# A two-layer edge network: fewer, larger transfers on the SyncE queue, with three blocks of the message table in one

## The chip, the cores and the metric

One core of one Trainium2 chip runs the kernel. The metric is device time in microseconds (us), smaller is better. The kernel before took 12610.75 us as the median of three runs (12586.5 to 12617.3).

## The reference

A graph has 12500 nodes with 128 features and 412500 directed edges, sorted by their target. Layer 0 weights and sums the source rows of every node's edges and passes the sum through a small network. Layer 1 computes a filter for every edge from its 50 attributes (two linear layers with softplus), multiplies it into a row of its *target* end and sums the products by its *source* end. Both layers end in a residual and a layer norm.

```python
# layer 0, on x, src, dst, w
agg = segment_sum(w[:, None] * x[src], dst)
x = layernorm(x + relu((x + agg) @ W1 + b1) @ W2 + b2)
# layer 1
h1 = x @ lin1_w.T
c = 0.5 * (cos(w * pi / 10) + 1)
f = softplus(attr @ nn_w1.T + nn_b1) - log(2)
F = (softplus(f @ nn_w2.T + nn_b2) - log(2)) * c[:, None]
agg = segment_sum(F * h1[dst], src)
x = layernorm(x + (h1 + agg) @ lin2_w.T + lin2_b)
```

## The kernel before

Edges are cut into 403 tiles (T) of 1024 edges (TE), each of 8 groups (SUB) of 128, in two halves of 512 (HE). As the edges are sorted by target, a tile's targets lie in a window of 42 nodes (WIN), rarely in more than one.

The kernel runs in stages, each a block in which every engine has a program of its own, in order, and engines meet by semaphores. `wait_apart` is a semaphore wait followed by an increment of a counter of its own; `prime` is a tiny DMA that starts a semaphore off.

**First layer's edges** (lines 357 to 605). For each tile GpSimd gathers source rows with 8 indirect DMAs (line 433) into `xg`. TensorE sums them with a weighted one-hot (L473) into a window of `aggT`, which VectorE adds up (L498). The same loop prepares layer 1: TensorE multiplies the tile's attributes, `attr` (51 rows with a row of ones, two buffers of 512 edges), with the first filter matrix (L479), ScalarE makes the softplus (L396 to L400), VectorE puts it into `hid` (two buffers, L505), and SyncE stores it to `hidden` in HBM (L365). VectorE and TensorE also compute every edge's place in a table sorted by source bucket (buckets of 128 nodes). The edges form 4 parts; in each part a bucket has a run of whole blocks of 512 rows. The last block of a run is only partly filled, so SyncE clears a block for it ahead of time (L381). SyncE's program for one tile is: two loads of `attr`, two stores of `hid`, one clear. `PT` is 101 tiles, a part.

**First layer's nodes** (`layer0_nodes`) writes, among others, `h1_parts`: the rows of h1 as three bfloat16 parts (128 columns each) that add up to float32.

**Second layer's edges** (`layer1_edges`, from L944). For each tile, SyncE loads `e_hid` (two halves, L1009), the targets `dstb` (L1017, the same row for all partitions) and the window's h1 rows `h1w` (L1020): 3 x 42 rows, one DMA for each of the three parts, one part below the other. TensorE computes the second filter layer (L1077, L1080), ScalarE the softplus (L1135 to L1139), VectorE the one-hot `ohT` (L1223), TensorE picks and adds the three parts of h1 (`take_h1`, L1091), VectorE finishes the messages (L1238, L1245) and GpSimd scatters the message rows with 8 indirect DMAs into the sorted table (L1199). A table row has 132 numbers: the message, its place in the bucket, and its factor c.

105 tiles (`alone`) run like this. From then on, in the third loop (298 tiles, two to an iteration), a *turn* of three blocks (`TURN`) is summed beside each tile: SyncE reads their row numbers from `slot_row` (`find_blocks`, L1026), loads the three blocks (`load_blocks`, L1038, 264 KB each, into one of two sets of three buffers), VectorE and ScalarE build one-hots from the rows' places (L1273, L1167 and L1169), TensorE sums (`sum_turn`, L1111) and VectorE adds the sum into `aggT` (`add_turn`, L1285). The blocks of a turn always are neighbours in the table, and a turn never crosses a part. After the last tile some 90 turns follow, without tiles (the last loop).

SyncE's order for one tile of the third loop is: `load_hidden` (two waits on `z2_set`, two DMAs), `find_blocks` for the next turn (three register loads), `written` (two waits until scattered rows have landed), `load_blocks` (three times: a wait on `summed1`, so that the block's buffer is free, and a DMA), `load_windows` (a wait and the DMA of `dstb`, a wait and three DMAs of `h1w`). TensorE's order is: second filter layer, `take_h1`, `sum_turn`. VectorE's is: `ohT`, messages, then for each of the three blocks `add_turn`'s add and the next turn's one-hot. ScalarE's is: softplus, then the next turn's one-hots.

**Second layer's nodes** writes the output.

Of the kernel before, what the change touches and what calls it, by code (L numbers as in the profile page):

```python
# [51 lines left out]
def edge_network_kernel(nc, x_rows, x_cols, src_cols, dst_cols, w_cols, dst_rows,  # L52
# [8 lines left out]
    with ctx:  # L61
# [3 lines left out]
        def sem(name):  # L65
            return ctx.enter_context(nc.semaphore(name))
# [240 lines left out]
        with ExitStack() as c1:  # L307
# [3 lines left out]
            with ExitStack() as c2:  # L311
# [13 lines left out]
                attr = [sb2(f"attr{h}", [P, HE], f32) for h in range(2)]  # L325
                soft1 = [sb2(f"soft1_{h}", [P, HE], f32) for h in range(2)]
                hid = [sb2(f"hid{h}", [P, HE], f32) for h in range(2)]
# [12 lines left out]
                attr_padded, attr_in = sem("attr_padded"), [sem(f"attr_in{h}") for h in range(2)]  # L340
                z1_set, abs1, exp1, ln1, hid_set = (sem(n) for n in ("z1_set", "abs1", "exp1", "ln1", "hid_set"))
                hid_st = [sem(f"hid_stored{h}") for h in range(2)]
# [11 lines left out]
                with nc.Block() as block:  # L354
                    @block.sync
                    def _(sp):
# [5 lines left out]
                        def store_hidden(t, h):  # L362

                            wait_apart(sp, hid_set, taken_up(t, h), passed_sp)
                            sp.dma_start(hid_d[ds(t, 1), h, :, :].rearrange("o p e -> (o p) e"), hid[h][:, :]).then_inc(hid_st[h], 16)  # L365

                        for h in range(2):
                            prime(sp, spare[16 + h:17 + h, :], hid_st[h], zero)
                        sp.wait_ge(attr_padded, 2)
# [12 lines left out]
                        for h in range(2):  # L382
                            store_hidden(T, h)
                        for h in range(2):
                            sp.wait_ge(hid_st[h], 16 * (T + 2))
                        sp.wait_ge(blocks_cleared, 16 * T)
# [53 lines left out]
                    def _(pe):  # L440
# [16 lines left out]
                        for q, first, past_last in parts:  # L457
                            plan_part(q)
                            with pe.Fori(first, past_last) as t:
# [16 lines left out]
                                for h in range(2):  # L476
                                    pe.wait_ge(attr_in[h], 16 * (t + 1))
                                    pe.wait_ge(hid_set, taken_up(t, h))
                                    nc.tensor.matmul(bank[2 + h][:, :], nn1[:, :], attr[h][:, :], start=True, stop=True).then_inc(z1_set, 1)  # L479
# [966 lines left out]
```

## Time and profile before

| | us |
|---|---|
| median of three runs | 12610.75 |
| the profiled execution | 12679.28 |
| its span, first to last instruction | 12677.7 |
| PE busy | 6363.2 (50%) |
| DVE busy | 6551.5 (52%) |
| ACT busy | 4527.6 (36%) |
| POOL busy | 6390.3 (50%) |

PE is TensorE's matmuls, PEld its weight loads, DVE VectorE, ACT ScalarE, POOL GpSimd and SP SyncE. `SPq` is SyncE's sequencer, which issues DMAs. A span covers one core. The granted TensorE clock had a mean of 0.64 of full speed, and the DMA engines moved 121 GB/s over the span. A wait is put down to what released it; "remote" stands where an update came late that the profile can't put down to an instruction just before it.

### The profile page before, as it was taken

The numbers are of one execution on the slowest core, as the hardware profiler recorded it, in microseconds if no ns is written. First come the engines' busy times: TensorE is split into PE (matmuls) and PEld (weight loads), VectorE is DVE, ScalarE is ACT, GpSimd is POOL, SyncE is SP. The second block draws the span as 40 slices with busy tenths as digits, with TensorE's granted clock in tenths as the row PEclk, the third lists the DMA queues.
The fourth block names the chain that finished last, engine by engine and source line by source line (L and its number), as shares of the span: only waits on it lengthen the run. The fifth ranks groups of instructions, "written<-read, shape, count | busy, mean of one in ns | idle before, by whom it ended". The sixth has DMA issues, their size and how long they took to land. (4 is left out here: it accounts for less than half of the span.)

```text
span 12677.7 us, 208085 instructions
## 1 busy us (share of the span) xinstructions
PE 6363.2 (50%) x29276; PEld 4956.9 (39%) x29548; DVE 6551.5 (52%) x18326; ACT 4527.6 (36%) x9921; POOL 6390.3 (50%) x6542
## 2 busy tenths in 40 slices
PE   2555566655665555553333444444444444444457
PEld 1333333333333333343333344444444444444457
DVE  7666666666666555543333344444444444444457
ACT  2333333333333333343333333333333333333347
POOL 3666666566666666625555444444444444444430
PEclk7555555555555555575565666666666666666678
DMA  3333333333333333333333444444444444444456
GB/s 99 117 118 118 116 121 120 116 120 116 121 118 120 119 114 117 116 121 99 100 101 100 123 123 123 123 123 124 123 122 123 124 122 124 124 122 122 122 151 202
DMA packets 864996, 1531.32 MB, mean 121 GB/s; under 512 B 235294, under 2 KB 249044, under 8 KB 864460
## 3 DMA queue, kind: packets, MB, share of 16 engines
q1 hardware_dynamic: 655168, 1091.59, 28.2%
q0 software_dynamic: 209456, 436.16, 11.6%
q10 hardware_dynamic: 348, 3.33, 0.1%
q14 instruction: 18, 0.15, 0.0%
q8 instruction: 6, 0.10, 0.0%
HBM read 967.92 MB, written 562.42 MB: 121 GB/s over the span
## 5 line engine op out<-in xcount | busy, mean ns | idle before, releaser
L1199 POOL DMA_INDIRECT sorted_messages<-rows,sidx x3224 | 3101.1, 962 | 3756.4 <-DVE sidx L1241 1776.6
L433 POOL DMA_INDIRECT xg<-x_rows,gidx x3224 | 3247.3, 1007 | 2118.2 <-issue 1040.1
L473 PE MATMUL bank<-onehot,xg 128*128 128x42 f32 x6448 | 1564.2, 396 | 1546.0 <-DMA xg<-x_rows,gidx 649.6
L473 PEld LDWEIGHTS bank<-onehot,xg 128*128 128x128 f32 x6448 | 1366.1, 298 | 1742.2 <-issue 972.4
L1091 PE MATMUL bank<-h1w,ohT 128*128 128x128 bf16 x3224 | 398.4, 301 | 3123.7 <-DMA h1w<-h_parts 1680.3
L479 PE MATMUL bank<-attr,nn 128*128 128x512 f32 x1612 | 1551.8, 1101 | 552.3 <-DMA attr<-attr_cols 402.9
L1111 PE MATMUL bank<-hot,block_rows 128*128 128x128 f32 x9312 | 1656.8, 357 | 41.3 <-DVE hot L1273 18.3
L1111 PEld LDWEIGHTS bank<-hot,block_rows 128*128 128x128 f32 x9312 | 1614.9, 270 | 56.1 <-issue 41.1
L1091 PEld LDWEIGHTS bank<-h1w,ohT 128*128 128x128 bf16 x3224 | 306.4, 137 | 3193.6 <-DMA h1w<-h_parts 3162.3
L1080 PE MATMUL bank<-w_nn2T,e_hid 128*128 128x128 f32 x6448 | 1044.0, 314 | 680.3 <-DMA e_hid<-hidden 606.7
L1080 PEld LDWEIGHTS bank<-w_nn2T,e_hid 128*128 128x128 f32 x6448 | 1004.1, 226 | 641.5 <-DMA e_hid<-hidden 547.2
L396 ACT ACTIVATE soft<-bank 128x512 f32<-128x512 f32 x808 | 477.0, 590 | 2152.1 <-remote 1254.6
L1135 ACT ACTIVATE soft<-bank 128x512 f32<-128x512 f32 x806 | 481.1, 597 | 2045.3 <-remote 1790.3
L1223 DVE TENSOR_SCALAR ohT<-dstb,rel 128x1024 bf16<-128x1024 int16 x403 | 199.6, 495 | 1935.1 <-DMA dstb<-dst 1770.3
L1167 ACT ACTIVATE hot<-cols,block_rows 128x128 f32<-128x128 f32 x1167 | 467.2, 400 | 1769.9 <-remote 875.7
L1273 DVE TENSOR_SCALAR hot<-neg_cols,block_rows 128x128 f32<-128x128 f32 x3501 | 1018.8, 359 | 4.6 <-DMA block_rows<-sorted_messages 4.6
L1285 DVE TENSOR_TENSOR aggT<-aggT,bank 128x128 f32 x1164 | 329.3, 283 | 1079.0 <-remote 715.7
L479 PEld LDWEIGHTS bank<-attr,nn 128*128 128x128 f32 x1612 | 447.4, 319 | 1068.4 <-issue 862.9
L1238 DVE SCALAR_TENSOR_TENSOR filt<-bank,soft 128x512 f32<-128x512 f32 x806 | 555.7, 689 | 550.3 <-ACT soft L1139 370.7
L1245 DVE TENSOR_TENSOR rows<-filt,bank 128x512 f32<-128x512 f32 x806 | 553.9, 687 | 401.3 <-remote 302.2
L561 DVE TENSOR_TENSOR onehot<-cols,rel 128x336 f32<-128x336 f32 x403 | 203.0, 504 | 971.6 <-remote 904.8
L412 ACT ACTIVATE gidx<-srci 128x4 int32 x806 | 165.5, 205 | 1401.5 <-DMA xg<-x_rows,gidx 820.3
(184 smaller groups left out, 8712.5 us busy)
## 6 DMA issues: line engine op xcount, KB each, us to landing
block_rows<-sorted_messages SPq DMA_DIRECT2D x1167, 264.0 KB
hidden<-hid SPq DMA_DIRECT2D x808, 256.0 KB
e_hid<-hidden SPq DMA_DIRECT2D x806, 256.0 KB
sorted_messages<-zero SPq DMA_DIRECT2D x403, 264.0 KB
dstb<-dst SPq DMA_DIRECT2D x403, 256.0 KB
attr<-attr_cols SPq DMA_DIRECT2D x806, 102.0 KB
xg<-x_rows,gidx POOLq DMA_INDIRECT x3224
sorted_messages<-rows,sidx POOLq DMA_INDIRECT x3224
```

The source lines that it names most:

```text
L396: nc.scalar.activation(soft1[h][:, :], bank[2 + h][:, :], ACT.Abs).then_inc(abs1, 1)
L433: pool.indirect_dma_start(xg[s][:, :], None, x_rows, bass.IndirectOffsetOnAxis(ap=gidx[s // HALF][:, s % HALF:s % HALF + 1], axis=0),).the ...
L473: nc.tensor.matmul(bank[0][:, 0:WIN], xg[s][:, :], onehot[:, s, :], start=(s == 0), stop=(s == SUB - 1)).then_inc(summed, 1)
L479: nc.tensor.matmul(bank[2 + h][:, :], nn1[:, :], attr[h][:, :], start=True, stop=True).then_inc(z1_set, 1)
L1080: ins = nc.tensor.matmul(bank[2 + h][:, s * P:s * P + P], hid[h][:, s * P:s * P + P], nn2T[:, :], start=False, stop=(s == HALF - 1))
L1091: ins = nc.tensor.matmul(bank[4 + h][:, s * P:s * P + P], ohT[:, at:at + P], h1w[:, :], start=True, stop=True)
L1111: ins = nc.tensor.matmul(sums[u][:, 0:P], block_rows[k][u][:, s, 0:D], hot[u][:, s, :], start=(s == 0), stop=(s == HALF - 1))
L1135: nc.scalar.activation(soft2[h][:, :], bank[2 + h][:, :], ACT.Abs).then_inc(abs2, 1)
L1199: pool.indirect_dma_start(table, bass.IndirectOffsetOnAxis(ap=sidx[h][:, s:s + 1], axis=0), rows[h][:, s, :], None).then_inc(landed[h], 16)
L1238: dve.scalar_tensor_tensor(filt[h][:, :], bank[2 + h][:, :], 0.0, soft2[h][:, :], ALU.max, ALU.add).then_inc(filt_set, 1)
L1245: dve.tensor_tensor(rows[h][:, :, 0:D], filt[h][:, :].rearrange("p (s d) -> p s d", s=HALF), bank[4 + h][:, :].rearrange("p (s d) -> p s d ...
L1273: ins = dve.tensor_scalar(hot[u][:, s, :], neg_cols[:, :], mine[:, s, D:D + 1], mine[:, s, D + 1:D + 2], ALU.is_equal, ALU.mult)
```

## The change

The pairs of buffers `attr`, `hid` and `e_hid` become one buffer each with the halves side by side, loaded or stored in one DMA; a set of three blocks becomes one buffer, loaded in one DMA from the first block's row; the three parts of the h1 rows come in one DMA with a rearranged source. Waits are on the later half, or on the third block's sum. Since a turn's three blocks are now read even where only the first is used, two more blocks behind each part's last are cleared, in four DMAs at the end of the first layer's edges. TensorE's matmuls, VectorE's and ScalarE's operations are the same apart from the waits and the buffers' names.

```diff
@@ first layer's edges, SyncE
-                        def store_hidden(t, h):
-
-                            wait_apart(sp, hid_set, taken_up(t, h), passed_sp)
-                            sp.dma_start(hid_d[ds(t, 1), h, :, :].rearrange("o p e -> (o p) e"), hid[h][:, :]).then_inc(hid_st[h], 16)
+                        def store_hidden(t):
+
+                            wait_apart(sp, hid_set, taken_up(t, 1), passed_sp)
+                            sp.dma_start(hid_d[ds(t, 1), :, :, :].rearrange("o h p e -> p (o h) e"), hid[:, :, :]).then_inc(hid_st, 16)
...
-                                for h in range(2):
-                                    wait_apart(sp, z1_set, made(t, h), passed_sp)
-                                    sp.dma_start(attr[h][0:GAUSS + 1, :], attr_cols[:, ds(t * TE + h * HE, HE)]).then_inc(attr_in[h], 16)
-                                for h in range(2):
-                                    store_hidden(t, h)
+                                wait_apart(sp, z1_set, made(t, 1), passed_sp)
+                                sp.dma_start(attr[0:GAUSS + 1, :, :].rearrange("a h e -> a (h e)"), attr_cols[:, ds(t * TE, TE)]).then_inc(attr_in, 16)
+                                store_hidden(t)
...
+                        store_hidden(T)
+                        for q in range(PARTS):
+
+                            sp.reg_load(end, ends[0:1, q * PT + NB:q * PT + NB + 1])
+                            row = sp.snap(end, min_val=0, max_val=TABROWS - BLOCK)
+                            sp.dma_start(sorted_d[q // TABLE_PARTS][ds(row, 2 * BLOCK), :].rearrange("(k p g) d -> p k (g d)", k=2, p=P),
+                                         zero[:, :].rearrange("p (o e) -> p o e", o=1).broadcast_to([P, 2, 4 * RW])).then_inc(blocks_cleared, 16)
@@ first layer's edges, TensorE and VectorE
-                                    pe.wait_ge(attr_in[h], 16 * (t + 1))
+                                    pe.wait_ge(attr_in, 16 * (t + 1))
...
-                            dve.wait_ge(hid_st[h], 16 * (t + 1))
+                            dve.wait_ge(hid_st, 16 * (t + 1))
@@ second layer's edges, SyncE
-                for h in range(2):
-                    wait_apart(sp, z2_set, freed(j, h), passed_sp)
-                    sp.dma_start(hid[h][:, :], hid_d[ds(t + 1, 1), h, :, :].rearrange("o p e -> (o p) e")).then_inc(hid_in[h], 16)
+                wait_apart(sp, z2_set, freed(j, 1), passed_sp)
+                sp.dma_start(hid[:, :, :], hid_d[ds(t + 1, 1), :, :, :].rearrange("o h p e -> p (o h) e")).then_inc(hid_in, 16)
...
-                    for k in range(3):
-                        sp.dma_start(h1w[WIN * k:WIN * (k + 1), :], h1_parts[ds(node, WIN), k * D:(k + 1) * D]).then_inc(h1w_in, 16)
+                    sp.dma_start(h1w[0:KEEP, :], h1_parts[ds(node, WIN), :].rearrange("r (k d) -> k r d", k=3)).then_inc(h1w_in, 16)
...
             def find_blocks(c, k):
-                for u in range(TURN):
-                    sp.reg_load(at[u], slot_row[0:1, ds(first_slot(c, k) + u, 1)])
+                sp.reg_load(at, slot_row[0:1, ds(first_slot(c, k), 1)])
...
-                for u in range(TURN):
-                    row = sp.snap(at[u], min_val=0, max_val=TABROWS - BLOCK)
-                    if used:
-                        wait_apart(sp, summed1, first_slot(c, k) + u + 1 - TURN, passed_sp)
-                    sp.dma_start(block_rows[k][u][:, :, :].rearrange("p g d -> p (g d)"),
-                                 table[ds(row, BLOCK), :].rearrange("(p g) d -> p (g d)", p=P)).then_inc(block_in[k][u], 16)
+                row = sp.snap(at, min_val=0, max_val=TABROWS - TURN * BLOCK)
+                if used:
+                    wait_apart(sp, summed1, first_slot(c, k), passed_sp)
+                sp.dma_start(block_rows[k][:, :, :, :].rearrange("p u g d -> p u (g d)"),
+                             table[ds(row, TURN * BLOCK), :].rearrange("(u p g) d -> p u (g d)", u=TURN, p=P)).then_inc(block_in[k], 16)
@@ second layer's edges, VectorE (ScalarE's hot_turn alike)
-                dve.wait_ge(block_in[k][u], 16 * (c + 1))
+                if u == 0:
+                    dve.wait_ge(block_in[k], 16 * (c + 1))
```

## Rows read from the trace of the kernel before

**Rows 1.** stages: us, busy PE, PEld, DVE, ACT, POOL, PEclk, DMA share, GB/s

```profile
166.00:5377.00 5211.00, 3086.12 (x8865) 1886.88 (x8865) 3373.24 (x6670) 1619.48 (x3209) 3235.53 (x3213) 0.56 0.38 118
...
5573.00:7010.00 1437.00, 519.45 (x2637) 454.60 (x2741) 455.67 (x1589) 452.31 (x1065) 807.31 (x840) 0.59 0.33 101
...
7010.00:12246.00 5236.00, 2281.28 (x14698) 2206.89 (x14845) 2131.25 (x8014) 2013.20 (x4742) 2285.61 (x2376) 0.69 0.42 123
...
12246.00:12574.00 328.00, 282.49 (x2192) 267.69 (x2192) 275.50 (x1097) 235.42 (x553) 8.15 (x9) 0.97 0.73 225
```

**Rows 2.** waits of the third loop: us in total, times, longest

```profile
DVE ohT L1223 <- DMA dstb<-dst: 1534.1, 276, 11.2
...
PE bank L1091 <- DMA h1w<-h_parts: 1476.3, 159, 10.7
...
DVE aggT L1285 <- remote: 712.8, 145, 10.6
```

**Rows 3.** timeline of one tile: start us, us, engine, line, operation, idle before

```profile
9000.29 4.64 PE L1111 MATMUL bank<-hot,block_rows 128*128 128x128 f32 x24
...
9001.75 0.96 POOL L1199 DMA_INDIRECT sorted_messages<-rows,sidx  x1 [6.22 <-ACT rows L1146]
...
9005.26 7.94 SPq L1038 DMA_DIRECT2D block_rows<-sorted_messages  x3
...
9011.92 0.29 DVE L1285 TENSOR_TENSOR aggT<-aggT,bank 128x128 f32 x1 [5.85 <-remote]
...
9013.55 0.34 SPq L1017 DMA_DIRECT2D dstb<-dst  x1
...
9016.68 0.49 DVE L1223 TENSOR_SCALAR ohT<-dstb,rel 128x1024 bf16<-128x1024 int16 x1 [3.55 <-DMA dstb<-dst]
...
9020.57 0.96 POOL L1199 DMA_INDIRECT sorted_messages<-rows,sidx  x1 [9.02 <-DVE sidx L1241]
```

**Rows 4.** timeline of the tile behind it

```profile
9018.22 4.23 PE L1111 MATMUL bank<-hot,block_rows 128*128 128x128 f32 x24
...
9029.46 0.96 POOL L1199 DMA_INDIRECT sorted_messages<-rows,sidx  x1 [0.30 <-issue]
...
9032.29 0.60 ACT L1135 ACTIVATE soft<-bank 128x512 f32<-128x512 f32 x1 [7.93 <-remote]
...
9034.33 0.69 DVE L1238 SCALAR_TENSOR_TENSOR filt<-bank,soft 128x512 f32<-128x512 f32 x1 [3.15 <-ACT soft L1139]
...
9036.72 0.96 POOL L1199 DMA_INDIRECT sorted_messages<-rows,sidx  x1 [6.30 <-ACT rows L1146]
```

**Rows 5.** one line of SyncE in the third loop: ns min/median/max

```profile
L1038 SPq MOVE block_rows<-sorted_messages x891: 3/29/1396, 7012.5 to 12239.3; - x179
```

**Rows 6.** first layer's edges: waits, then two places of SyncE's timeline

```profile
PE bank L479 <- DMA attr<-attr_cols: 402.9, 154, 5.4
...
3003.05 7.07 SPq L375 DMA_DIRECT2D attr<-attr_cols  x2
...
3015.68 0.95 SPq L375 DMA_DIRECT2D attr<-attr_cols  x2
```

**Rows 7.** waits of the second layer without sums

```profile
PE bank L1091 <- DMA h1w<-h_parts: 194.1, 31, 13.3
```

**Rows 8.** DMA queue from 12300 to 12550, and the timeline of the last loop

```profile
q1 hardware_dynamic: 31717, 59.55, 78.3%
...
12403.12 1.01 SPq L1038 DMA_DIRECT2D block_rows<-sorted_messages  x2
...
12404.20 2.98 PE L1111 MATMUL bank<-hot,block_rows 128*128 128x128 f32 x24 [0.22 <-DVE aggT L1285]
...
12407.68 4.50 PE L1111 MATMUL bank<-hot,block_rows 128*128 128x128 f32 x33 [0.50 <-DVE hot L1273]
...
12405.96 0.40 ACT L1167 ACTIVATE hot<-cols,block_rows 128x128 f32<-128x128 f32 x1 [0.26 <-DMA block_rows<-sorted_messages]
```

**Rows 9.** DMA queue in the microsecond 9033 to 9034

```profile
q1 hardware_dynamic: 112, 0.02, 10.3%
```

More of the change, by code:

```diff
@@ L324, in edge_network_kernel @@
                 hits = sb2("hits", [P, PART_COLS], bf16)
-                attr = [sb2(f"attr{h}", [P, HE], f32) for h in range(2)]
+                attr = sb2("attr", [P, 2, HE], f32)
                 soft1 = [sb2(f"soft1_{h}", [P, HE], f32) for h in range(2)]
-                hid = [sb2(f"hid{h}", [P, HE], f32) for h in range(2)]
+                hid = sb2("hid", [P, 2, HE], f32)
                 cnt_i, blocks_i = sb2("bucket_rows_i", [P, 1], i32), sb2("bucket_blocks_i", [P, 1], i32)
@@ L486, in _ @@
                         dve.sem_inc(bucket_counts, NB)
-                        for h in range(2):
-                            dve.memset(attr[h][:, :], 0.0).then_inc(attr_padded, 1)
+                        dve.memset(attr[:, :, :], 0.0).then_inc(attr_padded, 1)
                         def wide(ap, n):
@@ L952, in layer1_edges @@
     ALU, ACT, ds = mybir.AluOpType, mybir.ActivationFunctionType, bass.ds
-    hid = [sbuf(f"e_hid{h}", [P, HE], f32) for h in range(2)]
+    hid = sbuf("e_hid", [P, 2, HE], f32)
     soft2 = [sbuf(f"soft2_{h}", [P, HE], f32) for h in range(2)]
@@ L961, in layer1_edges @@
     off, away, aside = (sbuf(n, [P, SUB], f32) for n in ("off", "away", "aside"))
-    block_rows = [[sbuf(f"block_rows{k}{u}", [P, HALF, RW], f32) for u in range(TURN)] for k in range(2)]
+    block_rows = [sbuf(f"block_rows{k}", [P, TURN, HALF, RW], f32) for k in range(2)]
     hot = [sbuf(f"hot{u}", [P, HALF, P], f32) for u in range(TURN)]
     sums = [bank[0], bank[1], bank[6]]
-    hid_in = [sem(f"hid_in{h}") for h in range(2)]
+    hid_in = sem("hid_in")
     dstb_in, h1w_in = sem("dstb_in"), sem("h1w_in")
@@ L971, in layer1_edges @@
     passed, passed_sp = sem("e_passed_pool"), sem("e_passed_sp")
-    block_in = [[sem(f"block_in{k}{u}") for u in range(TURN)] for k in range(2)]
+    block_in = [sem(f"block_in{k}") for k in range(2)]
     hotD_set, hotA_set, dist_set, summed1, added = (sem(n) for n in ("hotD_set", "hotA_set", "dist_set", "summed1", "added"))
@@ L997, in _ @@
             jobs = TileTable(sp, "sp1", nwin, base)
-            at = [sp.alloc_register(f"sp1_block_row{u}") for u in range(TURN)]
+            at = sp.alloc_register("sp1_turn_row")
             begun = [sp.alloc_register(f"sp1_begun{k}") for k in range(4)]
@@ L1086, in take_h1 @@
                 pe.wait_ge(oh_set, j + 2)
[L1087 removed]
+                pe.wait_ge(h1w_in, 16 * (j + 1))
                 pe.wait_ge(msg_set, freed(j, h))
@@ L1110, in sum_turn @@
                     for s in range(HALF):
-                        ins = nc.tensor.matmul(sums[u][:, 0:P], block_rows[k][u][:, s, 0:D], hot[u][:, s, :],
+                        ins = nc.tensor.matmul(sums[u][:, 0:P], block_rows[k][:, u, s, 0:D], hot[u][:, s, :],
                                                start=(s == 0), stop=(s == HALF - 1))
```

32 lines of the change are left out of this document (14 added, 18 removed).

## The prediction

> **What bounds the kernel now.** I read the stages first [rows 1]. The profiled execution took 12679.28 us (span 12677.7), 68.5 us above the median of the three timed runs (12610.75). Four loops make up nearly all of it: the first layer's edges (403 tiles in 5211 us, 12.93 us a tile), the second layer's edges without sums (105 tiles in 1437 us, with the start of the stage), the same with sums (298 tiles in 5236 us, 17.57 us a tile) and sums alone (90 turns in 328 us). No engine is busy for more than two thirds of any of the first three, and the DMA engines for at most 0.42, so waits bound them.
>
> Next come the waits of the third loop [rows 2], then one pair of its tiles in order of time [rows 3, 4]. GpSimd scatters a tile's messages in eight indirect DMAs, 0.96 us each and 0.30 us apart, in one burst of 9.8 us (from 9001.75 to about 9011.55). What counts is the gap until the next burst. The reader is to see that the other engines stand still for the later part of a burst. TensorE's sums end at 9004.93 (9000.29 + 4.64), yet VectorE adds the last of them at 9011.92, 0.4 us after the burst, after 5.85 us of idle time put down to "remote": the update of `summed1` arrives only then. SyncE needs 7.94 us there to issue three block loads. How often: VectorE stood in this way for 712.8 us in 145 places [rows 2], so in about half of the 298 tiles. SyncE's shortest instruction shows the same: a MOVE has a median of 29 ns in this loop, but takes up to 1396 ns [rows 5]. I take from it that a SyncE instruction inside a burst costs about 0.7 us (7.94 us for some eleven of them), and that a semaphore update that isn't through some 2.5 to 3 us after the burst began is held to its end.
>
> So there are two kinds of tile. In the held kind [rows 3] the last block load waits for the held update, `dstb` is issued at 9013.55, `ohT` is built at 9016.68, and the next burst begins at 9020.57, 9.0 us after the last. In the other [rows 4] the burst ends at 9030.42, ScalarE gets its input, held as well, at 9032.29, VectorE gets the softplus at 9034.33, and the next burst starts at 9036.72: a gap of 6.3 us, ended by the softplus chain. There `h1w` arrives just in time.
>
> **The change part by part.** All sums are against the profiled time.
>
> 1. *Sums alone* (90 turns). Now a block may load as soon as its own third of the buffer is free. Afterwards 792 KB come in one DMA that waits for all three sums of the turn before. A load issued at 12403.12 releases ScalarE at 12405.96, 2.84 us later [rows 8]. Two blocks more in it cost from nothing (if its fixed part dominates) to 2 x 264 KB at 238 GB/s = 2.3 us. I take 1.6 us: 16 more packets for each of 16 engines at 99 ns (78.3% of 16 x 250 us over 31717 packets). So 0.15 us of wait and issue plus 4.4 us. After landing come VectorE's first one-hot and three blocks at the present pace (3.48 us for a turn, from 12404.20 to 12407.68, so 1.16 us each) with a fourth step to fill the chain: 4.3 us or so. The chain spans two turns, as there are two buffers: (0.15 + 4.4 + 4.3) / 2 = 4.4 us a turn, against 3.5 now. 90 x 0.9 = **+80 us** (bounds: with 2.84 us it is 3.65 a turn, +15 us; with 2.3 us more it is 4.8, +117 us).
>
> 2. *The third loop.* SyncE loses five of nine DMAs a tile (one of `e_hid`, two of the blocks, two of `h1w`), with their moves and waits, and two of three register loads. In a tile that isn't held the two spared `h1w` issues are worth 1.15 us. Of these about 0.5 us is lost to the larger `h1w` DMA, and the softplus chain lets only 0.25 us of the rest through: 153 x -0.25 = -38 us. The second block's instructions are hidden, since the wait for the third sum comes after them. In a held tile the one block DMA leaves after the burst, directly ahead of `dstb`, for which everything waits there. Now one block is ahead of it. Two more cost 1.3 us (bounds: 0, if they don't delay `dstb`; 2.3 us at 238 GB/s). The held share may change too: with `h1w` earlier, the sums start up to 0.4 us earlier against the burst, and their ends are spread around the limit (3.2 us after the start of a burst, held [rows 3]; 9018.22 + 4.23 against 9020.57, 1.9 us, not held [rows 3, 4]). I let a quarter of the 145 turn: 109 x 1.3 = +142, 36 x (6.3 - 9.0) = -97, 189 x -0.25 = -47. Together **0 us**; with no tile turned it is +150 us, with all turned -392 - 75 = -467 us.
>
> 3. *First layer's edges.* SyncE issues three DMAs a tile instead of five. TensorE waited for `attr` 402.9 us in 154 places. While gathers run, the two `attr` DMAs take 7.07 us to issue, otherwise 0.95 us [rows 6]; the second is what is late. One DMA leaves at the time of the first, with twice the rows' bytes. Most of those waits lie inside bursts, where TensorE's update would be held anyway. Outside them the spared issue of the `hid` store brings `attr` up to 0.7 us forward on TensorE's chain. I count a quarter of the 402.9 us: **-100 us** (bounds: all of it, -403 us; and +160 us, if the first half, no longer a DMA of its own, is 0.4 us late in all 403 tiles). The store of `hid` waits for both halves; VectorE needs the buffer again some 8 us later, so nothing waits for that.
>
> 4. *Second layer without sums.* TensorE waits for `h1w` 194.1 us in 31 places [rows 7], mostly on issues drawn out inside bursts; two of three go. Softplus inputs are held there as well. **-40 us** (bounds -194 us, and +74 us if the joined `e_hid` lands 0.7 us later for the first half in all 105 tiles).
>
> 5. *Four clears of two blocks* at the end of the first layer's edges: four issues and 4 x 528 KB behind the last store, 9.1 us at 238 GB/s, partly beside the other engines' last tile. **+5 us** (bounds 0 and +9). The single `memset` of `attr` runs once; the merged waits of ScalarE and VectorE stand beside their idle time.
>
> Sum: 80 + 0 - 100 - 40 + 5 = **-55 us**, 12624 profiled and 12555 in the timed runs.
>
> In the microsecond 9033 to 9034 only `h1w` is moved: 112 packets take 10.3% of 16 engines, so 15 ns each [rows 9]. The Trainium skill (DMA: Bandwidth & Descriptors, "Why a DMA increments its semaphore by 16 and not by 1") says that a DMA is split over the largest number of engines, up to 16, that divides the slowest dimension of both sides. By that rule 42 rows used 14 engines, and the new shape, 126 rows against 3 parts, uses 3: 42 rows on an engine instead of 9 in all. At 15 ns that is 0.5 us, as taken above. No view here shows the split itself.
>
> **The rivals.**
> - *Held tiles vanish.* If SyncE's lighter queue lets the sums get ahead of the limit, half to all of the 145 go to the 6.3 us gap. Half: 72 x -2.7 + 73 x 1.3 + 225 x -0.25 = -156 us, with the other parts -211, **12400**; all: -522, 12089. For it: less than 1 us decides in a tile. Against it: ScalarE's input stays held in both kinds.
> - *The big transfer stands in the way (slower).* Place: the SyncE queue just after a burst, in held tiles. Price: at 1.3 us and half of the gains of parts 3 and 4, 188 + 85 - 38 - 70 = +165, **12776**; at 2.3 us and no such gains, 333 + 85 - 38 = +380, 12991. It decides where the third sum's update comes after the burst and VectorE's wait for `dstb` (1534.1 us in 276 places [rows 2]) is the last one.
> - *All is hidden but the last loop.* SyncE's spared instructions lay beside held updates in every loop: 80 + 5, **12696**. For it: ScalarE's held input [rows 4].
> - *Few engines for `h1w`.* If a small row costs what a packet of a block costs (99 ns), 33 more on an engine are 3.3 us, less 1.15 us, in the 190 tiles where TensorE waited for `h1w` (159 and 31 [rows 2, 7]): +409 - 55, **12965**. The page's rule at its worst price; the 15 ns speak against it.
>
> **How the numbers follow.** The forecast has 0.45 (its own range 12450 to 12680), the vanished tiles 0.20, all hidden 0.15, the big transfer 0.14, few engines 0.06. A measurement of this kernel tells 0.3% (38 us) from no change. Of the forecast's 0.45, 0.27 is faster, 0.11 within, 0.07 slower; the vanished tiles are faster; of all hidden 0.03 is within and 0.12 slower; the other two are slower. That makes 0.47, 0.14 and 0.39. The range leaves a tenth on each side: 12330 to 12810.
>
> **What would show it.** Right: four SyncE DMAs a tile in the third loop; fewer than 145 "remote" waits of the add; a turn near 4.4 us in the last loop, with waits of VectorE or ScalarE for `block_rows`; `attr` waits well under 403 us. Wrong: a last loop that stays at 3.5 us a turn; a first loop that keeps its 12.9 us a tile; a third loop far from 17.6 us a tile either way; `h1w` waits that grow.

## The result and the profile after

The changed kernel took 11919.75 us (median of 4 runs, 11847.79 to 11946.0) beside 12598.62 us of the kernel before on the same chip: a ratio of 0.9453, interval 0.9407 to 0.9498. That is 679 us less; the forecast was 55 us less, and the range did not reach it. The profiled execution took 11847.79 us, 831.5 us less than the profiled one before.

The stages of the kernel after (columns as in [rows 1]; first layer, second layer without sums, third loop, sums alone):

```profile
163.00:5233.00 5070.00, 2908.76 (x8868) 1850.32 (x8869) 3380.04 (x6671) 1614.86 (x3210) 3257.62 (x3213) 0.59 0.39 122
5434.00:6821.00 1387.00, 550.32 (x2745) 466.13 (x2744) 454.89 (x1586) 442.87 (x1060) 809.81 (x839) 0.62 0.32 104
6821.00:11257.00 4436.00, 2377.81 (x14850) 2224.11 (x14850) 2158.87 (x8019) 1983.42 (x4752) 2298.88 (x2375) 0.74 0.46 145
11257.00:11743.00 486.00, 327.71 (x2192) 319.39 (x2192) 285.38 (x1101) 233.58 (x551) 11.49 (x12) 0.82 0.48 152
```

Against [rows 1] the first layer gained 141 us, the second layer without sums 50 us, the third loop 800 us (17.57 to 14.89 us a tile), and the last loop lost 158 us (3.6 to 5.4 us a turn, start and end included). So one term was wrong by 800 us. The waits of the third loop (us, times, longest) answer to [rows 2]:

```profile
ACT soft L1131 <- remote: 1138.3, 238, 9.0
...
PE bank L1087 <- DMA h1w<-h_parts: 770.5, 112, 9.9
...
DVE ohT L1220 <- DMA dstb<-dst: 506.6, 141, 7.2
...
DVE aggT L1283 <- remote: 175.4, 40, 10.6
```

ScalarE's line in the kernel before was

```profile
ACT soft L1135 <- remote: 1347.8, 268, 9.2
```

The held adds fell from 145 to 40, the wait for `dstb` to a third, that for `h1w` to half; ScalarE's held input fell by a sixth only. The timeline of one tile (start us, us, engine, line, operation, idle before) shows why, beside [rows 3, 4]:

```profile
9697.05 0.96 POOL L1196 DMA_INDIRECT sorted_messages<-rows,sidx  x1 [3.94 <-ACT rows L1142]
...
9697.37 0.38 SPq L1034 DMA_DIRECT2D block_rows<-sorted_messages  x1
...
9699.77 0.02 SPq L1016 DMA_DIRECT2D dstb<-dst  x1
...
9700.35 0.60 ACT L1131 ACTIVATE soft<-bank 128x512 f32<-128x512 f32 x1 [0.93 <-PE bank L1076]
...
9702.68 0.02 SPq L1018 DMA_DIRECT2D h1w<-h_parts  x1
...
9705.62 0.49 DVE L1220 TENSOR_SCALAR ohT<-dstb,rel 128x1024 bf16<-128x1024 int16 x1 [3.11 <-issue]
...
9707.16 4.08 PE L1107 MATMUL bank<-hot,block_rows 128*128 128x128 f32 x24
...
9708.59 0.60 ACT L1131 ACTIVATE soft<-bank 128x512 f32<-128x512 f32 x1 [3.25 <-remote]
...
9711.48 0.38 SPq L1034 DMA_DIRECT2D block_rows<-sorted_messages  x1
...
9711.69 0.96 POOL L1196 DMA_INDIRECT sorted_messages<-rows,sidx  x1 [4.75 <-DVE sidx L1238]
```

`dstb` leaves 2.7 us after the burst's start, `h1w` inside the burst, `ohT` is built before the burst's last DMA has ended, and TensorE is through with its sums at 9711.24, before the next burst begins. In [rows 3] `ohT` came 5.1 us after the burst. So the next block load and the next `dstb` leave in the first microseconds of the next burst too (9711.48 and 9712.40): being early hands itself on. ScalarE takes the first half of its input inside the burst, at 9700.35, and only the second half is held, to 9708.59; in [rows 4] both halves waited for the end of the burst.

I counted this for tiles 107 to 401 from the starts of `dstb` and the ends of the bursts: a tile is *late* when `dstb` is issued after the burst has ended. The kernel before has 196 late tiles of 295, the one after 41. A late tile's gap between bursts is 8.7 us on average before and 9.5 us after, any other's 5.7 and 4.2 us.

### The profile page after: what moved, and what is told of

Read it like the earlier page. It is cut to its first block and busy times, and to the rows that moved or that the text cites. A ratio compares the mean times of both kernels' runs of the same rounds, so it can differ in the third digit from the quotient of the medians.

```text
span 11846.2 us, 194081 instructions
## 1 busy us (share of the span) xinstructions
PE 6357.2 (54%) x29547; PEld 4997.1 (42%) x29548; DVE 6592.8 (56%) x18325; ACT 4480.2 (38%) x9921; POOL 6431.2 (54%) x6542
## 5 line engine op out<-in xcount | busy, mean ns | idle before, releaser
L474 PE MATMUL bank<-onehot,xg 128*128 128x42 f32 x6448 | 1480.5, 384 | 1775.0 <-DMA xg<-x_rows,gidx 881.2
L474 PEld LDWEIGHTS bank<-onehot,xg 128*128 128x128 f32 x6448 | 1303.3, 287 | 1940.3 <-DMA xg<-x_rows,gidx 979.3
L1107 PE MATMUL bank<-hot,block_rows 128*128 128x128 f32 x9312 | 1682.0, 362 | 174.2 <-DVE aggT L1283 156.5
L1107 PEld LDWEIGHTS bank<-hot,block_rows 128*128 128x128 f32 x9312 | 1640.9, 276 | 189.4 <-DVE aggT L1283 163.1
L480 PE MATMUL bank<-attr,nn 128*128 128x512 f32 x1612 | 1481.8, 1074 | 360.8 <-DMA attr<-attr_cols 335.4
L1076 PE MATMUL bank<-w_nn2T,e_hid 128*128 128x128 f32 x6448 | 1127.2, 329 | 994.8 <-DMA e_hid<-hidden 879.2
L1076 PEld LDWEIGHTS bank<-w_nn2T,e_hid 128*128 128x128 f32 x6448 | 1065.8, 239 | 1131.5 <-DMA e_hid<-hidden 967.9
L480 PEld LDWEIGHTS bank<-attr,nn 128*128 128x128 f32 x1612 | 484.3, 330 | 790.6 <-issue 607.6
```

The costliest lines, as they stand in the source:

```text
L474: nc.tensor.matmul(bank[0][:, 0:WIN], xg[s][:, :], onehot[:, s, :], start=(s == 0), stop=(s == SUB - 1)).then_inc(summed, 1)
L480: nc.tensor.matmul(bank[2 + h][:, :], nn1[:, :], attr[:, h, :], start=True, stop=True).then_inc(z1_set, 1)
L1076: ins = nc.tensor.matmul(bank[2 + h][:, s * P:s * P + P], hid[:, h, s * P:s * P + P], nn2T[:, :], start=False, stop=(s == HALF - 1))
L1107: ins = nc.tensor.matmul(sums[u][:, 0:P], block_rows[k][:, u, s, 0:D], hot[u][:, s, :], start=(s == 0), stop=(s == HALF - 1))
```

## The experiments

Eighteen runs were made, in five groups, each group on another chip; chip A is the one of the result. No chip was used for two groups. Every ratio is to the kernel before on the same chip. The chips turned out to be of two kinds, so the table comes first (third loop, last loop and late tiles of 295 from each run's trace, which is one execution):

| kernel | chip | ratio | third loop, us a tile | last loop, us | late tiles |
|---|---|---|---|---|---|
| before | A | 1 (12598.62 us) | 17.57 | 328 | 196 |
| changed | A | 0.9453 | 14.89 | 486 | 41 |
| three block DMAs | B | 0.9857 (0.9818-0.9895) | 17.30 | 325 | 190 |
| three h1w DMAs | B | 0.9889 (0.9852-0.9926) | 16.90 | 480 | 142 |
| two e_hid DMAs | B | 0.9694 (0.9644-0.9743) | 16.16 | 482 | 81 |
| first layer as before | B | 0.9666 (0.9632-0.9701) | 15.78 | 479 | 55 |
| changed, again | C | 0.9708 (0.9691-0.9726) | 16.26 | 484 | 86 |
| last loop in three | C | 0.9627 (0.9608-0.9647) | 16.38 | 324 | 88 |
| three DMAs, one wait | C | 1.0065 (1.0044-1.0085) | 18.05 | 349 | 266 |
| h1w rows interleaved | C | 0.9535 (0.9484-0.9586) | 15.25 | 480 | 26 |
| changed, third time | D | 1.0492 (1.0471-1.0513) | 12.13 | 483 | 0 |
| only the blocks | D | 1.0505 (1.0487-1.0522) | 12.26 | 482 | 0 |
| only h1w | D | 0.9996 (0.9987-1.0006) | 11.29 | 323 | 0 |
| 16 SyncE instructions | D | 1.0556 (1.0539-1.0574) | 12.29 | 479 | 0 |
| changed, fourth time | E | 0.9478 (0.9439-0.9517) | 15.02 | 481 | 32 |
| both edits | E | 0.9193 (0.9146-0.9241) | 14.65 | 324 | 21 |
| only the blocks | E | 0.9975 (0.9951-1.0000) | 16.71 | 483 | 130 |
| 16 SyncE instructions | E | 1.0117 (1.0089-1.0145) | 17.91 | 477 | 275 |
| only h1w | F | 1.0002 (0.9991-1.0013) | 11.17 | 322 | 0 |
| both edits | F | 1.0368 (1.0350-1.0386) | 12.05 | 322 | 0 |

The kernel before took 12696.21, 12743.45 and 12586.10 us on B, C and E, but 9559.26 and 9533.30 us on D and F. Its trace is there for A alone. On the four chips of the first kind the third loop's time goes with the late tiles, from 14.65 us with 21 to about 18 us with 266 and 275.

**Undoing one part (chip B).** The blocks first (this edit and those below are shortened; `row[u]` stands for the row that `at[u]` holds):

```
-                sp.reg_load(at, slot_row[.. first_slot(c, k) ..])
+                for u in range(TURN): sp.reg_load(at[u], slot_row[.. first_slot(c, k) + u ..])
-                if used: wait_apart(sp, summed1, first_slot(c, k), passed_sp)
-                sp.dma_start(block_rows[k][:, :, :, :] .., table[ds(row, TURN * BLOCK), :] ..).then_inc(block_in[k], 16)
+                for u in range(TURN):
+                    if used: wait_apart(sp, summed1, first_slot(c, k) + u + 1 - TURN, passed_sp)
+                    sp.dma_start(block_rows[k][:, u, :, :] .., table[ds(row[u], BLOCK), :] ..).then_inc(block_in[k][u], 16)
```

> The changed kernel with its three blocks loaded by three DMAs again, each with a wait and a register load of its own (the blocks' buffer and everything else as in the changed kernel). Theory (SyncE's queue): what SyncE issues in a tile of the third loop decides whether dstb and h1w leave before the GpSimd burst has slowed its instructions down; two DMAs, two loads and two waits more push dstb behind the burst again in many tiles. Then the third loop goes from 14.95 us a tile up to about 16.5 (+450 us), the last loop back from 5.15 to 3.4 us a turn (-158 us): together about +300 us against the changed kernel. Rival A (the joined h1w load alone made the gain): third loop stays near 15 us a tile, so -150 us. Rival B (the blocks alone made it): third loop back at 17.6 us a tile, +800 - 158 = +640 us.

The three `h1w` loads:

```
-  sp.dma_start(h1w[0:KEEP, :], h1_parts[ds(node, WIN), :].rearrange("r (k d) -> k r d", k=3)).then_inc(h1w_in, 16)
+  for k in range(3): sp.dma_start(h1w[WIN * k:WIN * (k + 1), :], h1_parts[ds(node, WIN), k * D:(k + 1) * D]).then_inc(h1w_in, 16)
```

> The changed kernel with the three parts of the h1 rows loaded by three DMAs again. Theory (SyncE's queue): two DMAs more a tile, issued last of a tile's loads; +1.4 us where they fall in a burst. Third loop +0.5 to +1 us a tile, +150 to +300 us, and the second layer without sums +20 to +50 us: +170 to +350 us together. Rival A (the joined h1w load made the gain): +700 us or more. Rival B (the blocks alone made it): within 50 us of the changed kernel, or faster by some tens of us, since the three DMAs spread over more engines.

The `e_hid` loads of the second layer:

```
-  wait_apart(sp, z2_set, freed(j, 1), passed_sp); sp.dma_start(hid[:, :, :], ..).then_inc(hid_in, 16)
+  for h in range(2): wait_apart(sp, z2_set, freed(j, h), passed_sp); sp.dma_start(hid[:, h, :], ..).then_inc(hid_in[h], 16)
```

> The changed kernel with the two halves of the first layer's rows (e_hid) loaded by two DMAs again in the second layer. Theory (SyncE's queue): one DMA and one wait more, ahead of all other loads of a tile, about half the price of two: +80 to +200 us over the two loops of the second layer. Rival (what counts is only what comes between the third sum and dstb): the e_hid load is issued beside waits, so nothing, within 40 us; and faster by up to 100 us if the joined transfer, for which both halves wait, is what now ends TensorE's wait for e_hid (606.7 us before, 879.2 us after).

The first layer's `attr` loads and `hid` stores, in the same way:

```
-  wait_apart(sp, z1_set, made(t, 1), passed_sp); sp.dma_start(attr[0:GAUSS + 1, :, :] ..).then_inc(attr_in, 16)
+  for h in range(2): wait_apart(sp, z1_set, made(t, h), passed_sp); sp.dma_start(attr[0:GAUSS + 1, h, :] ..).then_inc(attr_in[h], 16)
```

> The changed kernel with the first layer's attr and hid transfers in two DMAs each again. Theory: the first layer's loop goes back from 12.61 to 12.96 us a tile, +141 us, and nothing else moves. Rival (the first layer's gain came from the run, or from elsewhere, as the code's new place): within 40 us. It is worth more than the loop's own difference only if the first layer's stage also moves the second's, for which no row speaks.

The changed kernel didn't run on B, so only the order is firm. Without the joined blocks or the joined `h1w` most of the gain is gone, with 190 and 142 late tiles; the last loop goes back to 325 us with the blocks. That joined blocks or joined `h1w` alone made the gain (rivals A and B) falls: undoing either leaves about the same, 0.986 and 0.989. `e_hid` undone left 0.969, 52 us more than the first layer undone, but with no measure of the changed kernel on B its price can't be told. For the first layer alone nothing is settled here: its loop took 12.89 us a tile undone, 12.74 to 12.88 in the other three.

**One chip is not another (chip C).**

> The changed kernel once more, unaltered, so that the other kernels of this group can be set beside it on one chip. In the first group of experiments all four kernels, also the one that differs from the changed kernel in the first layer only, ran the third loop at 15.8 us a tile or more, against 14.95 us in the changed kernel's own profile. If that came of the chip, this run has a ratio near 0.965 and a third loop of 15.5 us a tile or more; if it came of the kernels, 0.945 and 15.0 us again.

It came of the chip, or of the hour on it: 0.9708, and 16.3 us a tile.

```
+   in the last loop only: three reg_loads; for u in range(TURN): wait_apart(sp, summed1, .. + u + 1 - TURN, ..)
+       sp.dma_start(block_rows[kk][:, u, :, :] .., sorted_d[TABLES - 1][ds(row[u], BLOCK), :] ..).then_inc(tail_in[kk][u], 16)
```

> The changed kernel, but in the last loop (sums alone) the three blocks are loaded by three DMAs with waits of their own, as before; the third loop keeps its one load. Theory: the loops don't touch one another, the last loop goes from 5.15 back to 3.4 us a turn, -158 us, and all else stays: 1.2 to 1.3% faster than the changed kernel. Rival: the last loop's code and its added waits also take time elsewhere, or the last loop was slow for another reason (the held clock, contention with the last scatters): then less than 80 us.

119.84 us less than the changed kernel by the medians of C, 160 us in the last loop's own time; the third loop was 36 us longer. The theory holds for the loop.

```
    for u in range(TURN):
-       if used: wait_apart(sp, summed1, first_slot(c, k) + u + 1 - TURN, passed_sp)
+       if used and u == 0: wait_apart(sp, summed1, first_slot(c, k), passed_sp)
```

> The changed kernel with three block DMAs and three register loads again, but with the changed kernel's single wait for all three sums ahead of them. Against the kernel with three DMAs and three waits (12504.68 us, ratio 0.986) it tells whether the number of SyncE's DMAs or the number and place of its waits counts. Theory (number of SyncE's instructions issued while a burst runs): near the three-wait kernel in the third loop, 17 us a tile or more (+600 us against the changed kernel), the last loop about 4.8 us a turn. Rival (the waits: three waits on summed1 that SyncE takes up one after the other, each seen late): near the changed kernel, within 100 us.

1.0065, 266 late tiles: the DMAs count, and where they stand. With three waits two of the three loads can leave before the third sum; with one wait all three stand between that sum and `dstb`, and it is 0.65% slower than the kernel before. Its last loop was expected at 4.8 us a turn and took 3.9:

```profile
12347.00:12696.00 349.00, 277.40 (x2179) 261.44 (x2180) 277.08 (x1097) 231.58 (x546) 7.68 (x8) 0.98 0.68 211
```

On this chip the last loop takes 324 us with three loads and three waits, 349 us with three loads behind one wait and 484 us with one load. So the joined wait costs 25 us, and 135 us come from joining the transfers: no block can be used before all three have landed.

```
-  sp.dma_start(h1w[0:KEEP, :], h1_parts[ds(node, WIN), :].rearrange("r (k d) -> k r d", k=3))
+  sp.dma_start(h1w[0:KEEP, :], h1_parts[ds(node, WIN), :].rearrange("r (k d) -> r k d", k=3))
   (and pidx, the row that a partition stands for, is p // 3 in place of p - 42k)
```

> The changed kernel with the rows of h1w laid out interleaved (row 3r+k in place of 42k+r; the one-hot's partition index is changed to match, at no cost in the loops), so that the one h1w DMA has 42 outer rows on both sides in place of 3 against 126. Theory (the joined h1w load is moved by few DMA engines and lands some 0.5 us later than it could): TensorE's wait for h1w (801.3 us in the profile after) shrinks, third loop -0.1 to -0.5 us a tile, -30 to -150 us. Rival (h1w is late by its issue, not by its transfer): within 30 us. Other rival (small descriptors are the same price however spread): the same.

245.8 us less than the changed kernel on C by the medians (1.8% by the ratios). TensorE's wait for `h1w` in the third loop, the changed kernel first:

```profile
PE bank L1087 <- DMA h1w<-h_parts: 1361.3, 163, 10.6
```

```profile
PE bank L1090 <- DMA h1w<-h_parts: 817.0, 136, 9.3
```

The gain is larger than the 30 to 150 us that I allowed, and not for the reason I gave. The issue on SyncE is shorter (ns min/median/max; changed kernel on D, then both edits on F):

```profile
L1018 SPq DMA_DIRECT2D h1w<-h_parts x288: 850/866/880, 5906.8 to 9399.6; - x144
```

```profile
L1023 SPq DMA_DIRECT2D h1w<-h_parts x289: 382/388/391, 5908.6 to 9392.5; - x145
```

and on D and F, where no burst is slow, TensorE's weight loads wait as long for `h1w` (1344.4 and 1374.9 us in all) and start 4.78 and 4.75 us after the issue on average, so it lands no earlier to speak of. On C the issue's median in the third loop fell from 722 to 388 ns, and 60 tiles moved from late to not late (86 to 26). That the shorter issue did this is a reading; no run there tells it from an earlier landing inside bursts.

**Where no burst is slow (chip D).**

> The changed kernel once more, as the measure for the other three of this group on their chip. Its ratio to the kernel before was 0.945 on one chip and 0.971 on another; if it lies with the chip and not with single executions, the four runs here agree within 1% and the ratio falls between 0.94 and 0.975.

> Of the change only the blocks' part (three blocks in one transfer, and the four clears of two blocks); h1w in three DMAs, e_hid, attr and hid in two, as in the kernel before. Theory (threshold: each step that SyncE spares before dstb and h1w moves tiles from 'dstb issued after the burst' to 'inside it', and the parts help each other): alone it brings the third loop from 17.6 to about 17.2 us a tile (-120 us) and costs 158 us in the last loop: ratio 0.99 to 1.005. Rival (the parts are independent, the blocks carry most): -400 us, ratio 0.965 to 0.975.

> Of the change only the h1w part (and the four clears). Theory (parts help each other): third loop from 17.6 to about 17.3 us a tile, -90 us, second layer without sums -20 us: ratio 0.985 to 0.995, and the gains of the parts alone add up to less than half of the whole change's. Rival (independent, h1w carries most): ratio 0.965 to 0.975. With few DMA engines as the mechanism (h1w lands later) it would be slower than before, above 1.00.

```
+                    for _ in range(8): sp.sem_inc(passed_sp, 1); sp.reg_mov(idle, 0)
                     wait_apart(sp, oh_set, j + 1, passed_sp)
                     sp.dma_start(dstb[:, :], dst16[ds(t, 1), :] ..
```

> The changed kernel with 16 instructions more on SyncE in each tile of the second layer, right before the wait for the one-hot that precedes dstb: 8 semaphore increments and 8 register moves, no DMA and no transfer. It tells whether it is SyncE's instructions or its DMAs that set dstb late. Theory (each SyncE instruction issued while GpSimd's burst runs takes about 0.7 us, and 0.03 us outside): 16 of them are up to 11 us inside a burst, so dstb falls behind the burst in most tiles and the third loop goes to 17.5 us a tile or more (+500 us or more over the changed kernel on this chip), dstb issued after the burst in over half of the tiles. Rival (only DMA issues or their transfers count): 16 instructions at 0.03 us, 0.5 us a tile at most, within 60 us.

Of the four only the rival of the last came true (57.4 us, "within 60"), and I did not expect such a chip: the kernel before took 9559.26 us, and the changed kernel was 4.9% slower. One line of SyncE in the third loop tells the kinds of chip apart (ns min/median/max): the changed kernel on A, then on D.

```profile
L1008 SPq MOVE e_hid<-hidden x295: 5/39/1393, 6824.5 to 11249.1; - x148
```

```profile
L1008 SPq MOVE e_hid<-hidden x294: 29/39/39, 5848.7 to 9438.8; - x147
```

On D no instruction of SyncE is drawn out, no wait of the third loop is "remote", and no tile is late. There the change has nothing to mend and its price shows. Beside the kernel with only `h1w` joined, which takes as long as the kernel before, it is 160 us in the last loop and 252 us in the third (12.13 against 11.29 us). The blocks' part alone brings it all (1.0505). In the third loop that price is, by the waits, `dstb` behind the big block load. The kernel with only `h1w` joined, then the changed one, both on D:

```profile
8003.83 2.28 SPq L1041 DMA_DIRECT2D block_rows<-sorted_messages  x3
8006.66 0.34 SPq L1021 DMA_DIRECT2D dstb<-dst  x1
...
8011.16 0.49 DVE L1226 TENSOR_SCALAR ohT<-dstb,rel 128x1024 bf16<-128x1024 int16 x1 [1.90 <-DMA dstb<-dst]
```

```profile
8007.40 0.38 SPq L1034 DMA_DIRECT2D block_rows<-sorted_messages  x1
...
8008.32 0.35 SPq L1016 DMA_DIRECT2D dstb<-dst  x1
...
8013.05 0.49 DVE L1220 TENSOR_SCALAR ohT<-dstb,rel 128x1024 bf16<-128x1024 int16 x1 [3.61 <-DMA dstb<-dst]
```

From the issue of `dstb` to `ohT` it is 4.50 us and 4.73 us in these tiles, and over the loop the waits are

```profile
DVE ohT L1226 <- DMA dstb<-dst: 501.4, 267, 3.7
```

```profile
DVE ohT L1220 <- DMA dstb<-dst: 812.2, 295, 4.8
```

311 us more. The mean delay from the issue of `dstb` to `ohT` is 4.15 and 4.73 us, so 0.6 us a tile is put down to the transfer ahead; `dstb` also leaves 0.4 us later after the start of the burst. The kernel with 16 instructions more bears this out: its `dstb` leaves 0.57 us later behind the block load, but `ohT` comes only 0.17 us later behind it. No run had `dstb` ahead of the blocks.

**The same on a chip with slow bursts (chip E).**

> The changed kernel as the measure for the other three of this group. If the chip is one with slow bursts (the kernel before near 12600 to 12750 us): ratio 0.945 to 0.971. If it is one without (before near 9560 us): 1.049 again, since then it is the chip and not the hour that decides.

> The changed kernel with two edits tried singly before: the last loop's three blocks in three DMAs (0.8% there over the changed kernel), and h1w's rows interleaved so that its one DMA has 42 outer rows on both sides (1.8%). Theory (the two touch different loops, so they add): 2.5% faster than the changed kernel where bursts are slow, 0.92 to 0.95 of before. Where they are not: -158 us for the last loop and nothing for h1w, 1.6% faster than the changed kernel, so still 1.03 of before. Rival (they don't add, h1w_spread's gain was one chip's scatter): 0.8% only.

> Of the change the blocks' part alone (and the four clears). Where bursts are slow: theory (parts help each other past a threshold): third loop between the kernel before and the changed kernel, nearer to before: 0.98 to 1.005. Rival (independent parts, blocks carry most): 0.955 to 0.975. Where they are not: 1.05 again.

> The changed kernel with 16 register and semaphore instructions more on SyncE ahead of the wait for dstb. Where bursts are slow: theory (each SyncE instruction in a burst costs about 0.7 us): dstb behind the burst in over half of the tiles, third loop 17.5 us a tile or more, +400 us or more over the changed kernel. Rival (only DMAs count): within 100 us. Where bursts are not slow: +57 us over the changed kernel again, since 16 instructions take 0.5 us.

Here are the two clearest results. The blocks alone gain nothing in all that can be told from zero (0.9975, interval to 1.0000). That is the net of two loops: against the kernel before on A the third loop is 0.86 us a tile shorter, 258 us, which is between the 120 us of the theory and the 400 us of the rival, and the last loop takes 155 us back. On B the joined blocks were worth 1.52 us a tile beside the other parts (17.30 against 15.78 us), so the parts help each other, as far as two chips can be compared. And the 16 instructions, 57 us on D, cost 827.7 us on E: SyncE's instructions set `dstb` late without any DMA. The rival (only DMAs count) falls. In one tile of that kernel:

```profile
9001.46 0.95 POOL L1200 DMA_INDIRECT sorted_messages<-rows,sidx  x1 [6.80 <-DVE sidx L1242]
...
9005.59 0.40 SPq L1038 DMA_DIRECT2D block_rows<-sorted_messages  x1
...
9013.93 0.01 SPq L1020 DMA_DIRECT2D dstb<-dst  x1
...
9015.95 0.49 DVE L1224 TENSOR_SCALAR ohT<-dstb,rel 128x1024 bf16<-128x1024 int16 x1 [9.23 <-DMA dstb<-dst]
...
9019.88 0.96 POOL L1200 DMA_INDIRECT sorted_messages<-rows,sidx  x1 [6.62 <-DVE sidx L1242]
```

8.3 us from the block load to `dstb`, where the changed kernel needs 0.92 us on D and 2.4 us in the tile of A above. Both edits together give 314.7 us over the changed kernel (2.6%; 2.5% expected): the fastest kernel of the study there.

**Two more (chip F).**

> Of the change the h1w part alone (and the four clears). Where bursts are slow (the kernel before near 12600 to 12750 us): theory (parts help each other past a threshold): 0.98 to 0.998, so that blocks and h1w alone together give less than half of the whole change's 0.948 to 0.971. Rival (independent parts; what the blocks don't give, h1w does): 0.955 to 0.975. Where they are not (near 9560 us): 1.000 again.

> The fastest version so far (last loop's blocks in three DMAs, h1w's rows interleaved) on one more chip. Where bursts are slow: 0.92 to 0.945 of the kernel before. Where they are not: the last loop gives back 158 us of the changed kernel's 472 us of loss, h1w's layout nothing, so 1.033.

F is like D. `h1w` joined alone is again no change, and both edits leave 1.0368 (1.033 expected). On such chips the kernel before stays the faster one. `h1w` alone was never run on a chip with slow bursts.

## Why the prediction was wrong

*What bounds it* held: slow SyncE instructions and held updates inside bursts, on this kind of chip. That the trace of before came from one of two kinds could not be seen in it.

*Step 2, third loop* (0 us forecast, -800 us measured) is the step that failed, in three places. First the share: "I let a quarter of the 145 turn". 105 of 145 held adds went. And held adds were the wrong thing to count: the kernel with three loads behind one wait has 68 of them and that with 16 instructions more, on E, has 33, yet both run at about 18 us a tile, with 266 and 275 late tiles. What decides is whether `dstb` leaves before the burst's end. I took the sums' end against the burst's start as fixed but for 0.4 us; but it is fed back, since an early `dstb` makes an early `ohT`, early sums and an early next `dstb`. On average the third sum ended 2.7 us after the next burst's start before and 0.7 us after it now; with the 16 added instructions it was back at 2.4 us.

Second the floor: the 6.3 us gap of [rows 4], from which I also had that a tile that isn't held gains only 0.25 us, was no floor. It is the gap of a tile whose ScalarE takes neither half of its input inside the burst. Before, 78 of the 99 tiles that are not late were so, at 6.4 us on average; 10 with one half taken had 4.3 us and 11 with both had 1.3 us. After, there are 64 of the first, 133 of the second and 57 of the third, at 5.9, 4.0 and 2.7 us. So the input that I took as held in both kinds of tile came free in most. The mean gap of tiles that are not late went from 5.7 to 4.2 us.

By the counts of late tiles: 155 tiles turned at 8.70 - 5.66 = 3.04 us are 471 us, and the 254 that are then not late, each shorter by 5.66 - 4.19 = 1.47 us, are 373 us; less 32 us, as the 41 that stay late are 0.77 us longer: 812 us, against the 800 us of the stages.

Third the price of the big load, 1.3 us a held tile for +142 us: right as a mechanism (0.6 us a tile where no burst is slow, bounds 0 to 2.3), but I had it paid by tiles that are held, and these went.

The rival *held tiles vanish* named the right thing and had a chance of 0.20; at its end, with all turned, it gave 12089 us. The measured 11919.75 us lie below, since the rival kept the 6.3 us and the 0.25 us.

*Step 1, last loop* (+80 forecast, +158 measured, over the bound of +117). The chain over two turns was 8.85 us; it is 10.2. On D the profile gives the landings of the last loop's loads:

```profile
DMA to landing us min/median/max: 4.3/4.5/5.6
```

4.4 was assumed. So the rest is 5.7 us, not 4.45. In the changed kernel on A VectorE waits once in two turns:

```profile
11500.93 0.86 DVE L1271 TENSOR_SCALAR hot<-neg_cols,block_rows 128x128 f32<-128x128 f32 x3 [1.82 <-DMA block_rows<-sorted_messages]
...
11502.10 5.11 PE L1107 MATMUL bank<-hot,block_rows 128*128 128x128 f32 x31 [2.60 <-DVE aggT L1283]
...
11506.66 3.04 SPq L1034 DMA_DIRECT2D block_rows<-sorted_messages  x2
...
11511.13 0.86 DVE L1271 TENSOR_SCALAR hot<-neg_cols,block_rows 128x128 f32<-128x128 f32 x3 [2.19 <-DMA block_rows<-sorted_messages]
```

10.2 us from one such wait to the next. VectorE starts at 11500.93 and the load for that buffer leaves at 11506.66: 5.7 us for a one-hot and three blocks, for which I had taken 4.3. The block's pace of 1.16 us was that of a pipe that never pauses. Here TensorE stood idle for 2.60 us, and the granted clock of the two microseconds behind that is 0.50, the lower level (1.2 GHz), and 1.00 again five microseconds later:

```profile
11502.00:11504.00 2.00, 1.90 (x9) 1.94 (x10) 1.73 (x7) 1.52 (x4) 0.00 (x0) 0.50 0.81 315
...
11507.00:11509.00 2.00, 2.00 (x19) 1.91 (x18) 0.98 (x4) 0.39 (x1) 0.00 (x0) 1.00 0.45 102
```

There 9 matmuls took 1.90 us, where 24 took 2.98 us before [rows 8]; over the loop the clock fell from 0.97 [rows 1] to 0.82. The mechanism was right, a chain over two turns through a larger load, and its second term was mis-sized: 5.7 us in place of 4.45.

*Step 3, first layer* (-100, measured -141 on A) was right in sign and near in size where bursts are slow. The waits for `attr` went from 402.9 us in 154 places [rows 6] to

```profile
PE bank L480 <- DMA attr<-attr_cols: 335.4, 77, 6.3
```

Half of the places are gone, but the time is less clear: kernels with the same joined load wait 288.4 to 421.7 us on C and E. On E it is 12.64 us a tile against 12.91 with the first layer's DMAs as before, -109 us. But kernels with the same joined transfers differ too, from 12.78 to 12.91 us a tile on C, so about 50 us of such a difference can be chance, and B settled nothing. On D it is the other way, 10.93 against 10.80, +52 us. That isn't the joined `attr` load of my bounds, since TensorE doesn't wait for `attr` in either kernel there; its wait for the gathered rows is longer (1662.1 against 1308.6 us), and why stays open.

*Step 4* (-40): -50 on A, and -53 on E against the kernel with only the blocks joined. On A the wait for `h1w` went from 194.1 us [rows 7] to 30.8, and TensorE's wait for `e_hid` rose (538.8 to 701.5 us). *Step 5* (+5) lies within what no run can tell; on D and F `h1w` joined with the same clears is 1.000.

The *big transfer* rival (slower) fell on A and is what happens on D and F: its place was right, behind the blocks' DMA, but it decides where no update is held, not where one is held. *All hidden but the last loop* fell, with three loops moved. *Few engines for `h1w`*: with the rows interleaved the landing did not move on F, and `h1w` joined alone cost nothing on D and F, so the price of 99 ns a row falls, and with it 12965 us. The 0.5 us of [rows 9] for the larger DMA can't be seen there either. The layout's 1.8% on C came another way.

## What to carry to other kernels

Where one late step makes the next one late, the cost of an instruction is not its time: find the moment from which it decides (here: is `dstb` issued before the burst slows the queue?), count the tiles on each side of it, and sum over the counts that the change would leave, not over those of before. Join transfers that stand between a late update and what all wait for; leave apart those whose parts are used one after the other, as the last loop's. To put the small transfer ahead of the big one is the next thing to try; no run here did. And before a sum is made from a trace, ask whether another chip would show the same phases: here the sign of the change hung on it.

## What the runs showed of the hardware

- Six chips ran the same kernel before at 12586 to 12743 us (A, B, C, E) and at 9533 to 9559 us (D, F), and what differs in their traces is what happens during the bursts of GpSimd's indirect DMAs: in the changed kernel's third loop a SyncE MOVE took up to 1393 ns on A and at most 39 ns on D, and VectorE's and ScalarE's waits on "remote" updates are there on A and missing on D. What makes a chip one or the other is open, and so is whether it stays so, since no chip came twice.
- On the slow kind 16 register and semaphore instructions a tile cost 827.7 us in the whole, on the other 57.4 us.
- A DMA issue on SyncE took 866 ns (median, D) with 3 outer rows at the source and 126 at the destination, and 388 ns (F) with 42 at the source. The Trainium skill (DMA: Bandwidth & Descriptors, "Why a DMA increments its semaphore by 16 and not by 1") gives 3 engines for the first and 14 for the second. The traces agree that the first is split less: they have 1605 updates of the load's semaphore for 403 loads on D and 5928 on F, 4.0 and 14.7 a load. The landing came no sooner.
- One load of 792 KB landed 4.5 us after its issue in the last loop on D (4.3 to 5.6). With three loads of 264 KB in that loop (F, both edits) the medians from each one's own issue are 2.8 to 3.4 us.
- In the last loop the granted clock was 0.97 to 0.98 with blocks in three loads (C) and 0.82 with one (A), where VectorE waits for a load 44 times in the 90 turns and TensorE pauses with it.
